# Written by parts: the first batch's split queries and keys on their way to the score operands

## The reference, cut to what matters

```
x = x + L0_attn(ln(x))   # 16 heads of 8; softmax over windows of 128, over tokens of the same index mod 4, and over all
x = x + L0_ffn(ln(x))    # 7 routed experts, top 2, and one shared
x = x + L1_attn(ln(x))   # 16 heads of 8, rotary positions, causal
x = x + L1_ffn(ln(x))    # 8 experts, top 2, one after the other, and a final layer norm
```

## Time and profile before

| | us |
|---|---|
| median of three runs | 1566.14 (1564.41 to 1570.2) |
| the profiled execution's own time | 1566.01 |
| its span, first to last instruction | 1564.2 |
| TensorE busy | 1379.2 (88%), mean granted clock 0.946 |
| VectorE busy | 1067.9 (68%) |
| ScalarE busy | 896.6 (57%) |
| GpSimd busy | 653.5 (42%) |

### The profile page before, as it was taken

How to read it: one execution, slowest core, us unless ns; L and a number is a source line. 1 busy time by engine, 2 the same in 40 slices (tenths; PEclk the granted TensorE clock), 3 DMA queues, 4 the chain that set the end, 5 groups by cost and what they waited for, 6 DMA issues and landing times. The chain is left out here.

```text
span 1564.2 us, 36776 instructions
## 1 busy us (share of the span) xinstructions
PE 1379.2 (88%) x12515; PEld 922.7 (59%) x12642; DVE 1067.9 (68%) x2706; ACT 896.6 (57%) x1595; POOL 653.5 (42%) x984
## 2 busy tenths in 40 slices
PE   4899999999999997998999992699999999973976
PEld 1355555555555554766999991255555555543976
DVE  4778778787877772674444444678887887745667
ACT  3567676767767665631444440356656666652776
POOL 3133233323423231146333317566667554252756
PEclk7799999999999998999999995699999999996988
DMA  5111211112121202370112112433433332313863
GB/s 156 48 51 35 64 53 44 56 36 70 30 62 42 62 5 73 91 109 10 47 49 49 49 39 31 112 71 73 125 74 95 77 86 67 92 39 101 262 175 99
DMA packets 91881, 113.78 MB, mean 73 GB/s; under 512 B 13108, under 2 KB 75475, under 8 KB 91699
## 3 DMA queue, kind: packets, MB, share of 16 engines
q1 hardware_dynamic: 74386, 89.33, 20.9%
q0 software_dynamic: 16736, 21.55, 6.0%
q10 hardware_dynamic: 576, 0.53, 0.1%
HBM read 71.91 MB, written 38.95 MB: 71 GB/s over the span
## 5 line engine op out<-in xcount | busy, mean ns | idle before, releaser
L533 DVE TENSOR_REDUCE wm<-wsm 128x16 f32<-128x512 f32 x512 | 330.6, 685 | 111.6 <-PE wsm L781 108.5
L967 ACT ACTIVATE we<-wst 128x1024 f32<-128x1024 f32 x320 | 325.1, 1023 | 117.2 <-PE wst L814 106.5
L529 DVE TENSOR_REDUCE cnm<-csm 128x1 f32<-128x512 f32 (+3 forms) x352 | 213.8, 637 | 47.6 <-PE csm L778 44.9
L967 ACT ACTIVATE ce<-cst 128x896 f32<-128x896 f32 (+1 forms) x256 | 173.5, 699 | 113.2 <-PE cst L809 77.0
L781 PE MATMUL wsm<-wks,wqs 96*128 96x512 bf16 x512 | 173.6, 395 | 11.7 <-DVE wm L533 6.2
L774 PE MATMUL csm<-cks,cqs 96*128 96x256 bf16 (+3 forms) x512 | 131.5, 309 | 13.4 <-DVE cnm L529 8.9
L814 PE MATMUL wst<-wqs,wks 128*128 128x512 bf16 x417 | 128.7, 383 | 13.2 <-issue 12.0
L2047 PE MATMUL abup<-abxt,abws 128*128 128x128 f32 x1120 | 139.0, 278 | 0.4 <-ACT abxt L2073 0.4
L2047 PEld LDWEIGHTS abup<-abxt,abws 128*128 128x128 f32 x1120 | 133.0, 195 | 0.7 <-ACT abxt L2073 0.7
L848 PE MATMUL woa<-we,wv 128*32 128x128 f32 (+2 forms) x2560 | 130.5, 340 | 0.0
L1077 POOL TENSOR_TENSOR wdif<-wglb,wloc 128x16 f32<-128x16 f32 x32 | 7.1, 221 | 288.9 <-DVE wloc L555 288.9
(11 more groups left out here) (321 smaller groups left out, 3006.8 us busy)
## 6 DMA issues: line engine op xcount, KB each, us to landing
wqs<-qk_parts SPq DMA_DIRECT2D x96, 96.0 KB
wks<-qk_parts SPq DMA_DIRECT2D x96, 96.0 KB
cqs<-qk_parts SPq DMA_DIRECT2D x96, 96.0 KB
cks<-qk_parts SPq DMA_DIRECT2D x96, 96.0 KB
br<-rows SPq DMA_DIRECT2D x39, 194.0 KB, 2.9
qk_parts<-wpt SPq DMA_DIRECT2D x48, 128.0 KB, 2.4
qk_parts<-cpt SPq DMA_DIRECT2D x48, 128.0 KB, 2.3
br<-rows SPq DMA_DIRECT2D x39, 130.0 KB, 3.0
```

What stands on the lines that cost most here:

```text
L529: dve.tensor_reduce(NM[:, n % 2, first:first + heads, t], got, AX.X, ALU.max).then_inc(s_mx, 1)
L533: dve.tensor_reduce(M[:, n % 2, hs, t, :].rearrange("p (w f) -> p w f", f=DIL), SM[:, j % 2, :].rearrange("p (w i f) -> p w f i", w=NT, f= ...
L967: act.activation(E[:, e_slot(g, i), 0:width], ST[:, (U * g + i) % 2, 0:width], ACT.Exp, scale=SCALE).then_inc(s_ex, 1)
```

## The change

Three edits, all to batch 0:

- `parts_out`: SyncE no longer waits for all three parts of a side before it writes the first. For batch 0 it waits for each part's own producer (`s_pa` at 1, at 2, then `s_pt`). Both attention stages.
- `k_first`, new, on ScalarE: the three key loads of the first head group are issued from ScalarE's queue, behind its wait for the three key part writes to have landed (`s_pw[1]`). SyncE's `stacks(0, 0)` returns after its query loads. In the window stage ScalarE does this between `values` and `xT` of batch 1, in the causal stage after the vcopy entries, ahead of `xT` of batch 1. Both stages.
- `ones`: in the window stage the memset of KS rows 64 to 95 is done by GpSimd behind `fill`, as float32 words (32 x 4096), in place of VectorE. The causal stage keeps VectorE's.

```diff
@@ PROLOGUE_W
-     ("values", 0, 1), ("norm_rows", 1), ("xT", 1), ...
+     ("values", 0, 1), ("k_first", 0), ("norm_rows", 1), ("xT", 1), ...
@@ PROLOGUE_C
-     ("vcopy", 0, 0), ("vcopy", 0, 1), ("norm_stats", 1), ...
+     ("vcopy", 0, 0), ("vcopy", 0, 1), ("k_first", 0), ("norm_stats", 1), ...
@@ VectorE
             def ones(b, turn, which):
                 if which == 0:
                     dve.memset(QS[64:P, :, :], 0.0).then_inc(s_ones, 1)
-                else:
-                    dve.memset(KS[64:P if causal else MR0, :, :], -1.0 if causal else 0.0).then_inc(s_ones, 1)
+                elif causal:
+                    dve.memset(KS[64:P, :, :], -1.0).then_inc(s_ones, 1)
@@ ScalarE
+            def k_first(b, turn):
+                act.wait_ge(s_ones, 2)
+                act.wait_ge(s_pw[1], 16 * SPLIT)
+                for a in range(SPLIT):
+                    act.dma_start(KS[a * SPLIT * DH:(a + 1) * SPLIT * DH, 0:HG, :], scratch[0, 1, :, 0:HG, :]
+                                  ).then_inc(s_rd[0], 16)
@@ GpSimd
+            def ones(b, turn, which):
+                if which and not causal:
+                    pool.wait_ge(s_init, 2 * NV)
+                    pool.memset(KS[64:MR0, :, :].rearrange("p h s -> p (h s)").bitcast(F32), 0.0).then_inc(s_ones, 1)
+                    pool.wait_ge(s_ones, 2)
@@ SyncE, parts_out
-                sp.wait_ge(s_pt[side], NPT * (b + 1))
+                if b:
+                    sp.wait_ge(s_pt[side], NPT * (b + 1))
                 ...
                 for a in range(SPLIT):
+                    if b == 0 and a < 2:
+                        sp.wait_ge(s_pa[side], a + 1)
+                    if b == 0 and a == 2:
+                        sp.wait_ge(s_pt[side], NPT)
                     sp.dma_start(scratch[b % 2, side, a * DH:(a + 1) * DH].rearrange("d h n -> h d n"),
                                  PT[:, side, a, :]).then_inc(s_pw[side], 16)
@@ SyncE, stacks, behind the query loads
+                if b == 0 and g == 0:
+                    return
```

More of the change, by code:

```diff
@@ L39 @@
      ("left2", 0, 1), ("ones", 0, 1), ("stacks", 0, 0), ("stacks", 0, 1), ("stacks", 0, 2), ("values", 0, 0),
[L40 removed]
+     ("values", 0, 1), ("k_first", 0), ("norm_rows", 1), ("xT", 1), ("vcopy", 0, 0), ("vcopy", 0, 1), ("proj", 1, 0),
      ("part1", 1, 0), ("proj", 1, 1), ("part1", 1, 1), ("left1", 1, 0), ("part2", 1, 0), ("left1", 1, 1),
@@ L52 @@
      ("left2", 0, 1), ("parts_out", 0, 1), ("stacks", 0, 0), ("stacks", 0, 1), ("stacks", 0, 2),
-     ("vcopy", 0, 0), ("vcopy", 0, 1), ("norm_stats", 1), ("norm_rows", 1), ("xT", 1), ("proj", 1, 0),
+     ("vcopy", 0, 0), ("vcopy", 0, 1), ("k_first", 0), ("norm_stats", 1), ("norm_rows", 1), ("xT", 1), ("proj", 1, 0),
      ("rot", 1, 0), ("join", 1, 0), ("part1", 1, 0), ("part2", 1, 0), ("proj", 1, 1), ("rot", 1, 1),
@@ L372, in slot @@
             return ev
-        SEQ = {"ones", "marks", "fill", "results", "early", "norm_stats", "norm_rows", "xT", "proj", "rot", "join", "part1", "left1", "part2", "left2",
+        SEQ = {"k_first", "ones", "marks", "fill", "results", "early", "norm_stats", "norm_rows", "xT", "proj", "rot", "join", "part1", "left1", "part2", "left2",
                "parts_out", "stacks", "values", "vcopy", "heads_T", "out_proj", "loads", "g_norm", "g_shift", "g_rows", "g_turn",
@@ L1032, in g_put @@
                                    ).then_inc(s_gwt, 1)
-            walk(act, dict(norm_rows=norm_rows, xT=xT, proj=proj, part1=part1, part2=part2, values=values, marks=ring_marks, maxima=maxima,
+            walk(act, dict(k_first=k_first, norm_rows=norm_rows, xT=xT, proj=proj, part1=part1, part2=part2, values=values, marks=ring_marks, maxima=maxima,
                            rows=rows, scores=scores, evac=evac, heads_T=heads_T, g_rows=g_rows, g_turn=g_turn, g_soft=g_soft,
@@ L1196, in scatter @@
                                         ).then_inc(s_sc[b % RING1], 16)
-            walk(pool, dict(results=results, early=early, fill=fill, norm_rows=norm_rows, join=join, left1=left1, left2=left2, vcopy=vcopy, sel=sel, maxima=maxima, scores=scores,
+            walk(pool, dict(ones=ones, results=results, early=early, fill=fill, norm_rows=norm_rows, join=join, left1=left1, left2=left2, vcopy=vcopy, sel=sel, maxima=maxima, scores=scores,
                             loads=loads, g_norm=g_norm, g_beta=g_beta, g_put=g_put, scatter=scatter))
```

## The result

The changed kernel takes 1562.05 us (median of 20 runs, 1559.18 to 1565.19) against 1565.83 us for the kernel before on the same chip (20 runs, 1563.81 to 1570.2): ratio 0.9974, 95% interval 0.9968 to 0.9979, so 3.8 us faster by the medians and 0.26% by the ratio (3.3 to 5.0 us by its interval). The forecast was 1562.3. That it lies 0.25 us from the median is finer than the measurement can tell, so that much of the agreement is luck.

A forecast was written before the change was run, and what follows sets the result against it. Each attention stage's start was taken to bind: in the window VectorE's memset holds the loads, which hold the first product. Window 3.8 us plus causal 0, off 1566.14, gave 1562.3 us; range 1559.5 to 1568.0.

The forecast's parts named there:

- VectorE's memset holds the loads, the loads hold the stage: Window stage: query loads wait for VectorE's memset until 25.55, the first product for the loads; the memset alone gives 2.57 us.
- Single writes add 1.2 us: Window stage: writing parts one by one starts the query loads another 1.2 us sooner, beyond the memset's 2.57.
- 9.17 us from first query load to first product, keys on a second queue or not: Window stage: this distance stays 9.17 us, as three DMA engines bound the loads and a second queue adds no speed.
- `k_first` gains nothing: Key loads on ScalarE's queue: alone at most the 1.25 us of issues; the forecast sum stays at 30.9.
- Out by 24.85: Window stage: the three key loads are issued from ScalarE by 24.85, the last key write having landed at 23.6.
- First product at 30.9: Window stage: first score product at 21.75 + 9.17 = 30.9 instead of 34.72, 3.8 us sooner.
- GpSimd's memset, 3.60 to 4.82 us, "I take the slower": Window stage: the moved memset takes 3.60 to 4.82 us on GpSimd, ends by 20.17 and costs nothing.
- Causal stage 0: Causal stage: query loads 1.3 us sooner, but VectorE takes nothing before 994.17; gain 0, at most 0.3 us.
- my mark for being wrong: Window stage: ScalarE's batch-1 copy, expected at 24.85, coming later than 25.5 would show the prediction wrong.
- The second queue loses its turn: Rival, chance 0.08: SyncE's next query loads are served before the keys, 3.9 us; window no gain, causal 2.6 lost, total 1568.5.
- All 3.8 us reach the end: Window stage: everything behind the first product is relative to it, so the whole 3.8 us reaches the stage's end.
- My other mark: First window product to causal stage's start: a distance changed by over 1 us would show the prediction wrong.

The follow-up runs named there:

- e1: Kernel before with only the window stage's memset of KS moved to GpSimd; ratio 0.9969 to the kernel before.
- e5: Changed kernel with the memset of KS back on VectorE, single part writes and ScalarE key loads kept; ratio 0.9989 to the kernel before.
- e2: Changed kernel with the first key loads back on SyncE's queue, single part writes and GpSimd's memset kept; ratio 0.9975 to the kernel before.
- e3: Changed kernel with part writes held back until all three parts of a side are there, as before; ratio 0.9984 to the kernel before.
- e6: Changed kernel with key part 2 made ahead of batch 1's statistics and batch 1's key projection behind the first sixteen products; ratio 0.9972 to the kernel before.
- e7: As e6, with nine query loads of 8 rows for the window's first group and ScalarE key loads in the window stage only; ratio 0.9954 to the kernel before.
- e8: As e7, with the first key loads behind the nine query loads on SyncE's queue; ratio 0.9952 to the kernel before.
- e9: The changed kernel itself, run again on one chip with e10; ratio 0.9967 to the kernel before, median 1563.54 us.
- e10: Changed kernel with all key loads on SyncE's queue, on one chip with e9; ratio 0.9961 to the kernel before, median 1561.48 us.
- e4: Kernel before with single part writes and ScalarE key loads in the causal stage only, window stage unchanged; ratio 0.9998 to the kernel before.

## Why the prediction was right

- *VectorE's memset holds the loads, the loads hold the stage*: right. e1 gives 2.7 us of product time for the memset alone (2.57 worked out), and e5 without it only 0.6. The device time alone would not have shown which part of the change pays: e1, e2 and the whole change can't be told apart by it.
- *Single writes add 1.2 us*: right at the product, 1.3 (e2 against e1 on one chip, 31.62 - 30.32). In the time it isn't seen: 0.9975 for e2, which has them, and 0.9969 for e1, which hasn't.
- *9.17 us from first query load to first product, keys on a second queue or not*: right, 9.02 to 9.23 in the seven runs of a changed kernel whose product waited for the keys, and 8.80 and 8.83 in e3 and e5. That the threefold loads set it is shown by e6 against e7 and e8. The 3.9 us for three loads at 74 GB/s is 4.0 when a KB is taken as 1024 bytes; nothing hung on it.
- *`k_first` gains nothing*: nothing speaks against it (e9 and e10). "Out by 24.85" was 25.41, since key part 2 was 0.5 us late in that profile and its three issues took 1.41 us instead of 1.25.
- *First product at 30.9*: 31.38, and 30.36 in e9. The term that was off is one that I took as fixed: the start of batch 1's statistics behind the late weights' landing, 19.27 in the trace before, 19.76 after, 18.7 to 18.9 in the experiments that have the same order, where the row names no DMA and the statistics follow within 0.2 us on VectorE's own work. It moves the change's gates and, before, the memset's too, so the difference between kernels is less touched: 3.34 us in the two profiles, 4.0 for e9 against e4 (on different chips); 3.8 was forecast, so it lies between the two.
- *GpSimd's memset, 3.60 to 4.82 us, "I take the slower"*: it took 3.50 to 3.51 in every run that has it, beside three VectorE subtractions; the slower row was no measure for it, nothing hung on it. By the Trainium skill ("SBUF — State Buffer", section "SBUF: two separate sides") VectorE work with two SBUF inputs contends only with GpSimd work that reads SBUF, which a memset doesn't. The 3.50 us agrees: it is 0.86 ns an element, as the 2.87 us of the memset of 3328 elements. Why the causal memset of 2048 elements takes 2.41 us, no run here shows.
- *Causal stage 0*: right (e4). The wait on ScalarE costs nothing there and 0.2 us in the window (the copy at 25.51, transposes done at 25.21, last key issue at 25.41); my mark for being wrong, a copy later than 25.5, was passed by 0.01, through the late weights and this 0.2 us.
- *The second queue loses its turn* did not happen: it would have put 3.9 us more between load and product, and where the next group's queries left right behind the first (after, e6, e9) there are 9.02 to 9.10. That the keys had gone a little sooner without them is not excluded.
- *All 3.8 us reach the end*: right within what the medians can tell (3.3 to 5.0). My other mark (the distance to the causal stage unchanged to 1 us) fell, by 1.3, and was badly chosen: that distance scatters by 2 us.

## What to carry to other kernels

When a load is the last gate, look at which gate holds its *issue*, and move that first: here a memset that any idle engine can do. A second queue gave no speed here, where the same few DMA engines carried both loads, and its wait stood in the way of the engine that issued it; it was harmless only when what it waited for was there before that engine's next work was due. A threefold repetition as outermost dimension held the loads to three engines, and removing it paid in full only when the engine behind the load was ready to take the data earlier.

## What the runs showed of the hardware

- Loads of 96 KB with a threefold repetition outermost moved at 74 GB/s with a DMA share of 0.18, three of sixteen engines. By the Trainium skill ("DMA: Bandwidth & Descriptors", section "Why a DMA increments its semaphore by 16 and not by 1") nine loads of 8 rows would use eight. The measured share is 0.37 to 0.40, some six on average; that they are short of eight because the loads come one by one fits the 93 GB/s of their issue, but wasn't tried.
- The three key loads took ScalarE 1.36 to 1.58 us to issue (single ones 0.30 to 0.62), SyncE 1.11 to 1.25, and ScalarE computed nothing meanwhile.
- The chip of e1 to e4 ran the kernel before in 1612.9 us instead of 1567.5. Its window stage was no slower (batch 0 ends at 140.9 us in e4, as before); e4's span is 49.6 us longer than that of the profile before, some 43 of it behind the last causal batch (its L611 at 1402.6 us before and 1408.9 in e4), in the last expert passes. Why, was not tried.
